# Experts 4 to 7 gated on ScalarE and added by GpSimd, experts 0 to 3 left on VectorE

## The chip, the core and the metric

The kernel runs on one core of a Trainium2 chip. The metric is the device time of one launch in microseconds (us); before the change it was 2887.42 us, the median of three runs (2886.21 to 2891.09). A core has five engines with instruction streams of their own: TensorE multiplies matrices, VectorE and ScalarE work on the 128 partitions of a tile, GpSimd does so more slowly and does not read the accumulation banks here, and SyncE issues the loads and stores. Streams meet in semaphores alone, and each engine takes its instructions strictly in order.

## The reference

Eight images of 128 channels and 48 x 48 positions (2304 tokens) go through one convolutional attention block and one transformer block.

```
x = x + conv_attention(groupnorm(x))        # q, k, v projections, softmax, squeeze-excite
t = tokens(x)
t = t + softmax(LN(t) LN(t)^T) LN(t)        # attention without weights
u = LN(t)
p = softmax(u @ router_w + router_b);  top_p, top_i = top_k(p, 2);  top_p /= sum(top_p)
t = t + sum over the two of top_p * (u @ expert_w[e] + expert_b[e])
```

The kernel computes all 8 experts of each token and weights them with a gate that is zero for the six that were not chosen. A product of two fp32 matrices is three matmuls, of high and low halves (`three`, lines 978 to 980), so nearly every product also costs one ScalarE pass (the high half) and one VectorE pass (the low half).

## The kernel before

The 2304 tokens of an image are 18 tiles of 128; three tiles make a block (384 tokens), so an image has six blocks. One list, `PLAN`, names all steps in order; every engine runs through it and does its own part of each step. So the list sets the order of work on all engines at once.

An image passes two stages. In the first (about 60 to 225 us of the trace for the first image) the scores of the convolutional attention are computed, and no expert step stands in it. In the second (`s1` steps) there are 54 slots. In slot w TensorE does `s1` (six matmuls), then `pv1` of slot w-2 (six matmuls); ScalarE takes the exponential of `s1` (L623) and its high half (L632); VectorE takes the low half (`p1low`, L866, out `pt_lo`). Each slot carries further steps (`beside`): the normalisation and projections of the next image (L530 and L765 for k, L537 and L777 for v), transposes of finished tokens (`o1t`, L873 to L881), and the expert layer of a finished block. For one block that is `uln` (mean and variance, L823 to L830, then a power of -0.5 on GpSimd, L497), one slot later `uapply` (L843, writes `u_tok`), one slot later `ut` (TensorE transposes `u_tok`, L991), one slot later `router`, then six expert steps in six slots, and `yt` (transpose of `acc`, out to memory) three slots after the last of them. The blocks' slots are in `MOE_SLOTS`; `uln` falls in slots 2, 10, 21, 30, 39 and 47, the expert steps in slots 6 to 11, 15 to 20, 26 to 31, 35 to 40, 44 to 49 and 52 to 57. Slots from 54 on are the start of the next image's first stage.

Of the kinds in `SOON` (experts and projections) a step stands ahead of `p1low` in its slot, all other steps behind it.

The six expert steps are two for each tile k: `("expert", b, m, k, 0)` for experts 0 to 3 and `(..., 1)` for experts 4 to 7. Here the first is called half A, the second half B; A stands in a block's first, third and fifth expert slot, B in the second, fourth and sixth. TensorE writes 512 columns (four experts) into one of two accumulation banks that take turns (`ring_bank`); it may write the bank again when the last reader of the step two places earlier on the ring is done (`wait_ring`, `LAST`). VectorE then runs four instructions of 128 columns a half (L951, L954), which alternate between two sums, `acc` and `acc_odd`, and at the end of B adds the two (L962).

## Time and profile before

| | |
|---|---|
| median of three runs | 2887.42 us |
| the profiled execution | 2888.97 us |
| its span in the trace | 2886.8 us |
| granted TensorE clock, mean | 0.98 |
| busy: TensorE, VectorE, ScalarE, GpSimd | 92%, 81%, 65%, 3% |

The profiled execution is 2.2 us longer than its span, and 1.55 us over the median. A busy share is the union of the instructions' spans. Instructions of one engine overlap: a VectorE instruction of 128 columns lasts 340 ns, but the next of a half starts 260 ns after it; matmuls overlap more. In a row of the timeline the first number is the start, the second the length, and a bracket at the end is the idle time of that engine before it and what ended it. Slots are counted here from the `s1` matmuls; rows of single slots are from the second image (b = 1), whose slot 0 begins at 565.8 us.

### The profile page before, as it was taken

How to read it: one execution, taken by the hardware profiler on the slowest of the kernel's cores; microseconds unless marked ns; L12 is line 12 of the kernel's file. 1: busy time of each engine (PE TensorE's matmuls, PEld its weight loads, DVE VectorE, ACT ScalarE, POOL GpSimd, SP SyncE). 2: the span in 40 equal slices, each digit the busy share in tenths (PEclk: the TensorE clock that was granted, in tenths of full speed). 3: DMA queues.
4: the chain of work that ended last, by engine and by line, in shares of the span. 5: the costliest groups of instructions: out<-in, count | busy, mean ns of one | idle time of the engine just before them, and what ended most of it. 6: DMA issues, size and time to landing. Idle time of an engine off the chain costs nothing.

```text
span 2886.8 us, 45014 instructions
## 1 busy us (share of the span) xinstructions
PE 2664.3 (92%) x15334; PEld 2388.0 (83%) x15334; DVE 2324.4 (81%) x6219; ACT 1882.9 (65%) x3729; POOL 90.1 (3%) x120
## 2 busy tenths in 40 slices
PE   5999999999899998999989999999999999899996
PEld 4888978889788897888878798888988889788885
DVE  4886888788887887878878788787888878888777
ACT  2777657666676666767567675676757767577662
POOL 0000000000000000000000000000000000000000
PEclk6999999999999999999999999999999999999998
DMA  1000000000000000000000000000000000000000
GB/s 34 1 1 17 7 6 1 17 7 6 6 1 18 6 6 6 1 18 6 9 4 1 17 7 12 1 1 17 9 9 1 1 20 6 9 1 1 4 9 11
DMA packets 10031, 23.00 MB, mean 8 GB/s; under 512 B 1992, under 2 KB 8528, under 8 KB 8784
## 3 DMA queue, kind: packets, MB, share of 16 engines
q1 hardware_dynamic: 9808, 20.14, 2.0%
q8 instruction: 126, 2.06, 0.3%
q14 instruction: 97, 0.79, 0.1%
HBM read 10.70 MB, written 9.44 MB: 7 GB/s over the span
## 4 chain that ended last, share of the span: by engine, by line
PE 51%; DVE 36%; ACT 6%; issue 6%; SPq 0%; DMA 0%; POOL 0%; ACTq 0%; DVEq 0%; POOLq 0%
PE ps L978 14%; PE ps L980 13%; PE ps L979 13%; PE ps L991 9%; DVE mx L782 6%; DVE pt_lo L866 5%; DVE acc L954 4%; DVE pt_lo L792 3%; DVE acc_odd L954 3%; ACT pt_hi L588 2%; ACT p_rows L576 2%; DVE u_tok L843 1%; DVE acc L962 1%; DVE t_tok L881 1%; ACT pt_hi L632 1%
## 5 line engine op out<-in xcount | busy, mean ns | idle before, releaser
L588 ACT ACTIVATE pt_hi<-ps 128x384 fp32r<-128x384 f32 x864 | 426.0, 493 | 319.7 <-PE ps L991 314.4
L792 DVE TENSOR_TENSOR pt_lo<-ps,pt_hi 128x384 fp32r<-128x384 f32 x864 | 479.2, 556 | 179.6 <-ACT pt_hi L588 171.4
L623 ACT ACTIVATE p_rows<-ps,shift 128x768 f32<-128x768 f32 x432 | 389.2, 901 | 236.7 <-PE ps L980 232.2
L576 ACT ACTIVATE p_rows<-ps,negmax 128x512 f32<-128x512 f32 (+1 forms) x720 | 465.4, 648 | 97.4 <-DVE negmax L786 90.7
L782 DVE TENSOR_REDUCE mx<-ps 128x1 f32<-128x512 f32 (+1 forms) x720 | 441.6, 632 | 70.6 <-PE ps L980 46.5
L991 PE MATMUL ps<-ident,p_rows 128*128 128x128 f32 x2736 | 456.6, 276 | 40.1 <-DVE pt_lo L792 22.9
L866 DVE TENSOR_TENSOR pt_lo<-p_rows,pt_hi 128x768 fp32r<-128x768 f32 x432 | 411.1, 952 | 85.8 <-ACT pt_hi L632 84.0
L991 PEld LDWEIGHTS ps<-ident,p_rows 128*128 128x128 f32 x2736 | 333.9, 141 | 153.1 <-issue 53.0
L632 ACT ACTIVATE pt_hi<-p_rows 128x768 fp32r<-128x768 f32 x432 | 365.5, 846 | 40.4 <-ACT p_rows L623 0.8
L978 PE MATMUL ps<-pt_hi,v_hi 128*128 128x384 f32 x864 | 358.3, 415 | 2.6 <-ACT y_out L597 2.6
L978 PE MATMUL ps<-xt_hi 128*128 128x384 f32 x864 | 306.7, 355 | 0.0
L978 PE MATMUL ps<-k_hi,q_hi 128*128 128x512 f32 (+1 forms) x720 | 277.9, 386 | 29.8 <-ACT p_rows L576 28.5
L978 PE MATMUL ps<-pt_hi,tn_hi 128*128 128x384 f32 x864 | 293.6, 340 | 9.8 <-ACT y_out L597 7.6
L980 PE MATMUL ps<-xt_hi,xt_lo 128*128 128x384 f32 x864 | 292.6, 339 | 0.0
L979 PE MATMUL ps<-xt_lo,xt_hi 128*128 128x384 f32 x864 | 292.4, 338 | 0.0
L980 PE MATMUL ps<-pt_hi,v_lo 128*128 128x384 f32 x864 | 291.5, 337 | 0.0
L980 PE MATMUL ps<-pt_hi,tn_lo 128*128 128x384 f32 x864 | 290.3, 336 | 0.0
L979 PE MATMUL ps<-pt_lo,v_hi 128*128 128x384 f32 x864 | 290.2, 336 | 0.0
L979 PE MATMUL ps<-pt_lo,tn_hi 128*128 128x384 f32 x864 | 290.0, 336 | 0.0
L979 PE MATMUL ps<-k_lo,q_hi 128*128 128x512 f32 (+1 forms) x720 | 273.3, 380 | 0.0
L980 PE MATMUL ps<-k_hi,q_lo 128*128 128x512 f32 (+1 forms) x720 | 272.8, 379 | 0.0
L978 PEld LDWEIGHTS ps<-pt_hi,tn_hi 128*128 128x128 f32 x864 | 163.0, 189 | 20.6 <-issue 13.0
(160 smaller groups left out, 4744.6 us busy)
## 6 DMA issues: line engine op xcount, KB each, us to landing
x_chan<-x SPq DMA_DIRECT2D x8, 1152.0 KB, 5.1
y<-y_out SPq DMA_DIRECT2D x48, 192.0 KB, 1.9
p_rows<-ew SPq DMA_DIRECT2D x1, 512.0 KB
p_rows<-eb SPq DMA_DIRECT2D x1, 512.0 KB
p_rows<-wq SPq DMA_DIRECT2D x1, 64.0 KB
p_rows<-wk SPq DMA_DIRECT2D x1, 64.0 KB
p_rows<-wv SPq DMA_DIRECT2D x1, 64.0 KB
w_sb<-w SPq DMA_DIRECT2D x2, 4.0 KB
```

What stands on the lines that cost most here:

```text
L576: act.activation(p_rows[:, ROW_BUFFER[r, n % 2], a:a + w], ps[:, c, 0:w], ACT.Exp, bias=negmax[:, r % 2:r % 2 + 1], accum_out=dparts[:, n, ...
L588: act.activation(pt_hi[:, slot, :], ring_bank(step)[:, 0:BW], ACT.Copy)\
L623: act.activation(p1_f[:, w % 2, :].rearrange("p (s w) -> p s w", s=2), ps[:, 2 * (w % 2):2 * (w % 2) + 2, 0:BW], ACT.Exp, bias=shift[:, :])\
L632: act.activation(p1_hi[:, w % 3, :], p1_f[:, w % 2, :], ACT.Copy).then_inc(p1_hi_ready, 1)
L782: link(dve.tensor_reduce(mx[:, c:c + 1], ps[:, c, 0:QC[c][1]], AX.X, ALU.max))
L792: dve.tensor_tensor(pt_lo[:, slot, :], ring_bank(step)[:, 0:BW], pt_hi[:, slot, :], ALU.subtract).then_inc(pt_lo_ready, 1)
L866: dve.tensor_tensor(p1_lo[:, w % 3, :], p1_f[:, w % 2, :], p1_hi[:, w % 3, :], ALU.subtract).then_inc(p1_lo_ready, 1)
L954: ins = dve.scalar_tensor_tensor(out=(even, odd)[i % 2], in0=term, scalar=gate, in1=total, op0=ALU.mult, op1=ALU.add)
L978: pe.matmul(out, lhs_hi, rhs_hi, start=start, stop=False)
L979: pe.matmul(out, lhs_hi, rhs_lo, start=False, stop=False)
L980: return pe.matmul(out, lhs_lo, rhs_hi, start=False, stop=stop)
L991: ins = pe.transpose(ring_bank(step)[:, k * 128:(k + 1) * 128], src(k), ident[:, :])
```

## The change

The B half becomes a step of its own kind, `scaled`, in the same slot. TensorE does what it did. VectorE has no part in it: it gates experts 0 to 3 of a tile (half A), two into `acc` and two into a second sum that now lies in `terms`. ScalarE multiplies each of experts 4 to 7 by its gate with one instruction (four of 128 columns) into `terms`, which lies in rows that the first stage uses. GpSimd then adds: term 0 + 1, term 2 + 3, `acc` + the second sum, (0+1) + (2+3), and the total into `acc`. `terms` has two places that tiles take in turns, so VectorE and ScalarE wait for the tile two before (`tile_added`). The bank of a B half is free when ScalarE is done (`terms_ready`), `yt` now waits for `tile_added`, and `scaled` stands in `SOON` as `expert` does.

```diff
-        s.setdefault(slot, []).append(("expert", b, m, i // 2, i % 2))
+        s.setdefault(slot, []).append((("expert", "scaled")[i % 2], b, m, i // 2))
...
+        terms = p_rows[:, 2, 0:2 * 5 * 128].rearrange("p (s a w) -> p s a w", s=2, a=5)
...
+                if kind == "scaled":
+                    m, k = step[2:]
+                    term = [terms[:, (m + k) % 2, i, :] for i in range(5)]
+                    total, paired = acc[:, k, :], at(terms_paired, *step) * 4 - 4
+                    pool.wait_ge(terms_ready, at(terms_ready, *step))
+                    pool.tensor_tensor(term[0], term[0], term[1], ALU.add).then_inc(terms_paired, 1)
+                    pool.tensor_tensor(term[2], term[2], term[3], ALU.add).then_inc(terms_paired, 1)
+                    pool.wait_ge(expert_added, at(expert_added, "expert", b, m, k))
+                    pool.tensor_tensor(total, total, term[4], ALU.add).then_inc(terms_paired, 1)
+                    pool.wait_ge(terms_paired, paired + 2)
+                    pool.tensor_tensor(term[0], term[0], term[2], ALU.add).then_inc(terms_paired, 1)
+                    pool.wait_ge(terms_paired, paired + 4)
+                    pool.tensor_tensor(total, total, term[0], ALU.add).then_inc(tile_added, 1)
...
+                elif kind == "scaled":
+                    m, k = step[2:]
+                    act.wait_ge(ring_full, filled(step))
+                    if k == 0:
+                        act.wait_ge(gates_ready, at(gates_ready, "router", b, m))
+                    earlier = tile_before(b, m, k, 2)
+                    if earlier:
+                        act.wait_ge(tile_added, at(tile_added, "scaled", *earlier))
+                    for e in range(E // 2):
+                        ins = act.activation(terms[:, (m + k) % 2, e, :], ring_bank(step)[:, e * 128:(e + 1) * 128],
+                                             ACT.Identity, scale=gates[:, m % 2, k, E // 2 + e:E // 2 + e + 1])
+                    ins.then_inc(terms_ready, 1)
...
+                    sums = acc[:, k, :], terms[:, (m + k) % 2, 4, :]
                     for e in range(E // 2):
...
-                    if half == 1:
-                        dve.wait_ge(vector_chain, chained(step, links[0]))
-                        dve.tensor_tensor(even, even, odd, ALU.add).then_inc(expert_added, 1)
...
-                    pe.wait_ge(expert_added, at(expert_added, "expert", b, m, TPB - 1, 1))
+                    pe.wait_ge(tile_added, at(tile_added, "scaled", b, m, TPB - 1))
```

VectorE, one image of the second stage, from the last half before `uln` to `uapply` of the same block (slots 39 and 40 of the first image). `u_raw`, `u_mv`, `u_ve` are the variance, `pt_lo` is `p1low`, `u_tok` is what `uapply` writes. Before:

```order
441 L866 TENSOR_TENSOR pt_lo<-p_rows,pt_hi 128x768
442 L823 BN_STATS u_raw<-t_tok 128x6 x3
443 L826 MEMSET wait_carrier 128x1
444 L828 BN_AGGR u_mv<-u_raw 128x2 x3
445 L830 TENSOR_SCALAR u_ve<-u_mv 128x3
446 L954 SCALAR_TENSOR_TENSOR acc<-ps,gates,acc 128x128
447 L954 SCALAR_TENSOR_TENSOR acc_odd<-ps,gates,acc_odd 128x128
448 L954 SCALAR_TENSOR_TENSOR acc<-ps,gates,acc 128x128
449 L954 SCALAR_TENSOR_TENSOR acc_odd<-ps,gates,acc_odd 128x128
450 L962 TENSOR_TENSOR acc<-acc,acc_odd 128x128
451 L866 TENSOR_TENSOR pt_lo<-p_rows,pt_hi 128x768
452 L843 TENSOR_SCALAR u_tok<-t_tok,u_mv,u_rs 128x128 x3
```

and in the changed kernel (L902 is the old L866, L859 to L866 the old L823 to L830, L879 the old L843):

```order
412 L902 TENSOR_TENSOR pt_lo<-p_rows,pt_hi 128x768
413 L859 BN_STATS u_raw<-t_tok 128x6 x3
414 L862 MEMSET wait_carrier 128x1
415 L864 BN_AGGR u_mv<-u_raw 128x2 x3
416 L866 TENSOR_SCALAR u_ve<-u_mv 128x3
417 L902 TENSOR_TENSOR pt_lo<-p_rows,pt_hi 128x768
418 L879 TENSOR_SCALAR u_tok<-t_tok,u_mv,u_rs 128x128 x3
```

The five instructions of half B between `u_ve` and `p1low` are gone. GpSimd, the same image around the power of `uln` in slot 47 (L518, the old L497), where before the powers of an image's blocks followed each other with nothing between:

```order
59 L515 TENSOR_TENSOR acc<-acc,p_rows 128x128
60 L508 TENSOR_TENSOR p_rows<-p_rows 128x128
61 L509 TENSOR_TENSOR p_rows<-p_rows 128x128
62 L511 TENSOR_TENSOR acc<-acc,p_rows 128x128
63 L513 TENSOR_TENSOR p_rows<-p_rows 128x128
64 L515 TENSOR_TENSOR acc<-acc,p_rows 128x128
65 L518 TENSOR_TENSOR u_rs<-u_ve,minus_half 128x3
66 L508 TENSOR_TENSOR p_rows<-p_rows 128x128
```

Rows 60 to 64 are the additions of the tile whose B half stands in slot 47 itself, so here the power is queued right behind them; for the other blocks the tile ahead of the power is of the slot before. ScalarE, slots 40 and 41 (L681 is the new instruction, L647 and L656 the old L623 and L632, L558 the old L537):

```order
326 L647 ACTIVATE p_rows<-ps,shift 128x768
327 L656 ACTIVATE pt_hi<-p_rows 128x768
328 L681 ACTIVATE p_rows<-ps,gates 128x128 x4
329 L647 ACTIVATE p_rows<-ps,shift 128x768
330 L656 ACTIVATE pt_hi<-p_rows 128x768
331 L558 ACTIVATE v_hi<-ps 128x384
```

The four new instructions stand behind the high half of their own slot and ahead of the exponential of the next.

## Rows read from the trace of the kernel before

**Rows 1.** The page: busy time and share of each engine.

```profile
PE 2664.3 (92%) x15334; PEld 2388.0 (83%) x15334; DVE 2324.4 (81%) x6219; ACT 1882.9 (65%) x3729; POOL 90.1 (3%) x120
```

**Rows 2.** Waits of TensorE, whole span: total us, times, longest.

```profile
PE ps L991 <- DVE u_tok L843: 58.0, 48, 4.1
```

**Rows 3.** Waits of TensorE from 589 to 735 us, second image.

```profile
PE ps L991 <- DVE u_tok L843: 4.5, 5, 1.3
PE ps L1008 <- DVE gs L718: 1.1, 1, 1.1
...
PE ps L978 <- DVE acc L962: 0.4, 1, 0.4
...
PE ps L1003 <- DVE gn_mv L710: 0.2, 1, 0.2
```

**Rows 4.** Waits of TensorE from 2708 to 2836 us, last image.

```profile
PE ps L991 <- DVE u_tok L843: 8.8, 5, 2.2
```

**Rows 5.** Timeline of VectorE, 693.5 to 699.3 us, slots 39 to 41.

```profile
695.63 0.17 DVE L830 TENSOR_SCALAR u_ve<-u_mv 128x3 f32<-128x3 f32 x1
695.71 0.35 DVE L954 SCALAR_TENSOR_TENSOR acc<-ps,gates,acc 128x128 f32<-128x128 f32 x1
...
697.08 0.95 DVE L866 TENSOR_TENSOR pt_lo<-p_rows,pt_hi 128x768 fp32r<-128x768 f32 x1
697.95 0.85 DVE L843 TENSOR_SCALAR u_tok<-t_tok,u_mv,u_rs 128x128 f32<-128x128 f32 x3
```

**Rows 6.** Timeline of TensorE, same stretch.

```profile
697.19 0.28 PE L979 MATMUL ps<-w_lo,xg_hi 128*128 128x128 f32 x1
697.30 0.27 PE L980 MATMUL ps<-w_hi,xg_lo 128*128 128x128 f32 x1
698.86 0.55 PE L991 MATMUL ps<-ident,u_tok 128*128 128x128 f32 x3 [1.28 <-DVE u_tok L843]
```

**Rows 7.** Timeline of ScalarE, same stretch.

```profile
692.82 0.91 ACT L623 ACTIVATE p_rows<-ps,shift 128x768 f32<-128x768 f32 x1 [0.96 <-PE ps L980]
693.82 0.85 ACT L632 ACTIVATE pt_hi<-p_rows 128x768 fp32r<-128x768 f32 x1
```

**Rows 8.** Timeline of VectorE and ScalarE, 637 to 641 us, slot 22.

```profile
638.33 0.61 DVE L765 SCALAR_TENSOR_TENSOR k_lo<-ps,biases,k_hi 128x384 fp32r<-128x384 f32 x1
```
```profile
637.51 0.56 ACT L530 ACTIVATE k_hi<-ps,biases 128x384 fp32r<-128x384 f32 x1
```

**Rows 9.** Timeline of VectorE and TensorE, slots 47 to 49.

```profile
721.99 0.34 DVE L954 SCALAR_TENSOR_TENSOR acc<-ps,gates,t_tok 128x128 f32<-128x128 f32 x1
...
723.89 0.85 DVE L843 TENSOR_SCALAR u_tok<-t_tok,u_mv,u_rs 128x128 f32<-128x128 f32 x3
```
```profile
724.80 0.55 PE L991 MATMUL ps<-ident,u_tok 128*128 128x128 f32 x3 [1.20 <-DVE u_tok L843]
```

**Rows 10.** Groups of ScalarE: shapes, count, busy us, mean ns.

```profile
L658 ACT ACTIVATE y_out<-ps,minus_one 128x384 f32<-128x384 f32 x48 | 27.3, 568 | 14.8 <-PE ps L991 14.8
L647 ACT ACTIVATE gexp<-centred 128x24 f32<-128x24 f32 x48 | 10.7, 223 | 91.6 <-DVE centred L900 91.6
```

**Rows 11.** Groups of GpSimd.

```profile
L497 POOL TENSOR_TENSOR u_rs<-u_ve,minus_half 128x3 f32<-128x3 f32 x48 | 41.5, 864 | 1235.6 <-DVE u_ve L830 1235.6
L465 POOL MEMSET ident<- 128x128 f32 x1 | 0.2, 204 | 0.3 <-POOLq L1174 0.3
L477 POOL TENSOR_SCALAR_AFFINE_SELECT group<-group 128x128 f32<-128x128 f32 x1 | 0.5, 523 | 0.0
```

**Rows 12.** Timeline of ScalarE and TensorE at the turn to the third image.

```profile
746.67 0.69 ACT L576 ACTIVATE p_rows<-ps,negmax 128x512 f32<-128x512 f32 x1 [4.13 <-DVE negmax L786]
```
```profile
747.50 0.50 PE L978 MATMUL ps<-k_hi,q_hi 128*128 128x512 f32 x1 [1.39 <-ACT p_rows L576]
```

**Rows 13.** Timeline of GpSimd and VectorE, 244 to 248 us.

```profile
245.15 1.56 POOL L494 TENSOR_TENSOR ln_rs<-ln_ve,minus_half 128x3 f32<-128x3 f32 x1 [23.20 <-DVE ln_ve L830]
```
```profile
245.04 0.96 DVE L866 TENSOR_TENSOR pt_lo<-p_rows,pt_hi 128x768 fp32r<-128x768 f32 x1
```

More of the change, by code:

```diff
@@ L122, in merge @@
         slots.setdefault(slot, []).extend(steps)
-SOON = ("expert", "kproj", "vproj", "qproj")
+SOON = ("expert", "scaled", "kproj", "vproj", "qproj")
 def first_stage(b):
@@ L378, in build @@
         expert_added = signal("expert_added")
+        terms_ready = signal("terms_ready")
+        terms_paired = signal("terms_paired")
+        tile_added = signal("tile_added")
         y_chan_ready = signal("y_chan_ready")
@@ L566, in take @@
                             act.wait_ge(o_added, at(o_added, "ot", b - 1, NB - 1))
+                        if n == 1 and r == 0 and b:
+                            act.wait_ge(tile_added, at(tile_added, "scaled", b - 1, 3, TPB - 1))
                         if n == 1 and r == 1 and b:
@@ L928, in take @@
                 elif kind == "expert":
-                    m, k, half = step[2:]
+                    m, k = step[2:]
                     dve.wait_ge(ring_full, filled(step))
-                    if k == 0 and half == 0:
+                    if k == 0:
                         dve.wait_ge(gates_ready, at(gates_ready, "router", b, m))
@@ L935, in take @@
                             dve.wait_ge(ring_full, filled(("yt", *block_before(b, m))))
-                    if half == 1:
-                        dve.wait_ge(expert_added, at(expert_added, "expert", b, m, k, 0))
-                    even, odd = acc[:, k, :], acc_odd[:, :]
+                    earlier = tile_before(b, m, k, 2)
+                    if earlier:
+                        dve.wait_ge(tile_added, at(tile_added, "scaled", *earlier))
+                    sums = acc[:, k, :], terms[:, (m + k) % 2, 4, :]
@@ L941, in take @@
                     for e in range(E // 2):
-                        i = half * (E // 2) + e
                         term = ring_bank(step)[:, e * 128:(e + 1) * 128]
-                        gate = gates[:, m % 2, k, i:i + 1]
+                        gate = gates[:, m % 2, k, e:e + 1]
                         if e >= 2:
                             dve.wait_ge(vector_chain, chained(step, links[0] - 1))
-                        if i == 1 and k:
-                            dve.wait_ge(expert_added, at(expert_added, "expert", b, m, k - 1, 1))
@@ L950, in take @@
-                        if i == 1:
-                            ins = dve.tensor_scalar(odd, term, gate, None, ALU.mult)
-                        else:
-                            total = residual(m, k) if i == 0 else (even, odd)[i % 2]
-                            ins = dve.scalar_tensor_tensor(out=(even, odd)[i % 2], in0=term, scalar=gate, in1=total,
+                        if e == 1:
+                            ins = dve.tensor_scalar(sums[1], term, gate, None, ALU.mult)
+                        else:
+                            ins = dve.scalar_tensor_tensor(out=sums[e % 2], in0=term, scalar=gate,
+                                                           in1=sums[e % 2] if e else residual(m, k),
@@ L1134, in take @@
                     ins.then_inc(ring_full, 1)
-                elif kind == "expert":
-                    m, k, half = step[2:]
+                elif kind in ("expert", "scaled"):
+                    m, k = step[2:]
+                    half = kind == "scaled"
                     wait_ring(step)
```

23 lines of the change are left out of this document (12 added, 11 removed).

## The prediction, made before the changed kernel was run

> **What bounds the kernel now.** The busy shares come first [rows 1]: TensorE 92%, VectorE 81%, ScalarE 65%, GpSimd 3%. So TensorE sets the time, and VectorE counts only where TensorE stands and waits for it. Next the waits of TensorE over the span [rows 2]: 58.0 us in 48 waits for `u_tok`, one per block. Then the same view cut to slots 9 to 53 of one image [rows 3]: 4.5 us for `u_tok` in five waits, 1.1 and 0.2 for the statistics of the next image (L718, L710), 0.4 for `acc`. The last image, which has no next one beside it, waits 8.8 us in its five [rows 4]. These sums are the ceiling, since the change leaves TensorE's own instructions alone. Last the timeline around one such wait, to see what `u_tok` is late for.
>
> **What is removed.** Of each of 144 tiles VectorE loses five instructions. In the timeline they begin at 695.71 and the next `p1low` at 697.08 [rows 5]: 1.37 us of VectorE a tile, 197 us in all (less than the 1.66 us of their added lengths, because they overlap). That is no gain by itself; the gain is what TensorE no longer waits. A wait that goes gives back a little more than its bracket: matmuls start 0.11 us apart but last 0.28 [rows 6], so I add 0.17 us to each.
>
> Slot 41. `u_ve` starts at 695.63, half B and `p1low` follow, `u_tok` starts at 697.95, and TensorE stands 1.28 us until 698.86 [rows 5, 6]. Without B halves VectorE is also no longer a slot behind: the high half of slot 40 is ready at 693.82 + 0.85 = 694.67 [rows 7], while VectorE takes it at 697.08. Ahead of `u_ve` the half B of slot 38 is gone as well: 695.63 - 1.37 = 694.3 at the earliest, and I allow 0.5 since VectorE now waits for its inputs, 694.8. Then 0.17 for `u_ve`, 0.86 for the power on GpSimd [rows 11] and 0.1 between engines: `u_tok` starts at 696.0 and lasts 0.85; TensorE is free for it from 698.86 - 1.28 = 697.6. The whole wait goes: 1.28.
>
> Slot 49. `u_tok` starts at 723.89, TensorE waits 1.20 us [rows 9]. Here half A of slot 48 stays. It began at 721.99 behind a late VectorE; I move it up by 1.1, to where its bank has just been filled, and `u_tok` with it, to 722.8. 1.0 of 1.20 goes, if the power is done by then.
>
> Slot 23. `k_hi` on ScalarE ends at 637.51 + 0.56 = 638.07 and `k_lo`, ahead of `u_tok` on VectorE, starts at 638.33 [rows 8]. VectorE is already up with ScalarE there, and no B half stands between. Only 0.2 of 0.93 us goes.
>
> Slots 12 and 32 hold the rest of the 4.5 us, 1.1 together; both have a half B in the slot of `uapply`. In slot 32 all goes, in slot 12 half: I take 0.9. The wait of 1.1 and the one of 0.2 for the statistics lie behind the same B halves of slots 9 and 11 and go, and the 0.4 for `acc` (a bank that a B half held) goes since ScalarE frees it.
>
> One full image: 1.28 + 1.0 + 0.2 + 0.9 + 1.1 + 0.2 + 0.4 = 5.1, and 6 waits x 0.17 = 1.0, so 6.1 us. Six images (b = 1 to 6): 36.6. The first image lacks slots 6 to 11 and their waits: 3.9. The last: its 8.8 us fall to a floor of about 1.8 (without projections there is less TensorE work ahead of the transposes, and `u_tok` cannot follow the high half faster), with the overlap 7.7. Sum 48.2 us.
>
> **What is added on ScalarE.** Four instructions of 128 columns from the bank, with the gate as a per-row scale. The trace has none; below stands 223 ns (24 columns, no per-row operand), above 568 ns (384 columns, with one) [rows 10]. On a line between the two 128 columns come to 0.32; I take 0.36, as the per-row operand costs the same at any width, and 1.3 us for four, 187 us in all, bounds 0.9 to 2.3. What hides it: ScalarE idles 0.96 us in a slot of 2.8 us until `s1` is done [rows 7], 1.9 in the two slots of a tile. The exponential of the next slot starts up to 0.4 us late and catches up in the next; `pv1` reads it two slots on. At 2.3 us the cover is gone, and each tile would cost up to 0.4: 58 us. I take 0.
>
> The Trainium skill ("ScalarE: Activation LUTs", What ACT_TABLE_LOAD costs) says 186 ns + 0.833 ns a column, 93 ns more for a per-row operand, and a 93 ns overlap. By its figures, an estimate, an instruction is 386 ns and four are 1.3 us; the sum would not move.
>
> **What is added on GpSimd.** Five additions a tile, 720 in all, of a kind that the trace lacks. Below: 204 ns, a fill of the same shape; above: 864 ns, the power of three columns; between them a select of 128 columns at 523 [rows 11]. I take 0.4, near the middle of fill and select, and with the two waits among them 2.2 us from the terms to `tile_added`. Bounds 1.1 to 4.5. Three places depend on it.
>
> First, a power behind additions in GpSimd's order. In four of the five the tile before is of the slot before and is done 3 us or more before `u_ve`. For slot 47 it is of the same slot: terms at about 719.3, additions until 721.5, power until 722.4, just ahead of the 722.8 above. Past 0.45 us an addition, this wait replaces the one removed.
>
> Second, the turn to the next image. There ScalarE idles 4.13 us for the row maximum (`negmax`), at the end of a run of halves and maxima on VectorE, until 746.67, and TensorE 1.39 us behind ScalarE until 747.50 [rows 12]. Three B halves leave this run; half A of the last tile and the last maxima are then held by TensorE filling their banks, and I put the exponential at 745.4, 1.3 earlier, not 3 x 1.37. But `yt` stands ahead of the second row of scores on TensorE and now needs the last addition: terms at 744.7, plus 2.2, so `yt` at 747.05 and the scores at 747.35. Of 1.3 us gained 0.15 are left, 1 us over seven turns.
>
> Third, the tail: the last tile's additions (2.2) replace a half and a sum on VectorE (1.37), +0.8 for each of two blocks, less some 0.8 for `u_tok` of the last block: +0.8, the turn at the end of the last image +0.4.
>
> **Contention.** In one row the power lasts 1.56 us and not 0.86; it begins 0.11 us after a `p1low`, which reads two operands from on-chip memory, and `u_tok` waits for it [rows 13]. So some pairs keep each other out. `p1low` fills a third of a slot; I charge 2 us for additions or `p1low`s that meet where it matters.
>
> The Trainium skill ("SBUF — State Buffer", Who interferes with whom) says that such a VectorE instruction and a GpSimd instruction that reads this memory exclude each other fully, whichever comes second waiting. The row agrees: 0.96 us of `p1low` ends 0.85 us into the power, and the power is 0.70 longer. By that rule VectorE's 432 `p1low`s could wait up to 0.4 us each; it is the second rival.
>
> The sum: 48.2 + 1.0 - 1.2 - 2.0 = 46 us. Against the profiled execution 2888.97 - 46 = 2843. The runs' median is 1.55 lower, 2841.4; I say 2841.5.
>
> **Rivals.**
>
> 1. The additions are slow, and the change loses. Place: GpSimd, ahead of `yt` and of the power of slot 47. At P us an addition the turn comes at 744.7 + 5P + 0.2; at P = 1.0 it costs 2.9 us in each of seven (20), slot 49 loses its gain and 1.8 more (22), the tail 5: 48 + 1 - 48, no change, 2888. From P = 1.1 on it is slower, at 1.3 by some 25 us, 2912. For it: no row has a GpSimd addition, and its 3-column power takes 0.86. Against: fills and selects of 128 columns take 0.2 to 0.5.
>
> 2. Exclusion costs more than 2 us. If each `p1low` in a slot with additions waits 0.4, VectorE still has room in most slots, but `u_tok` follows `p1low` directly: five blocks x 0.4 x 8 = 16 us, and additions stretched by one `p1low` (0.5 at the turn and in slot 47) 10 more. Gain 20, 2868. For: rows 13. Against: of 48 powers of `uln` the mean is 864 [rows 11], so few met.
>
> 3. More goes than I count: the waits of slots 12 and 23 go whole and the turn keeps 1.3 us (additions near 0.2). 1.1 an image and 8 at the turns: gain 63, 2825. Against: rows 8 show slot 23 bound by ScalarE.
>
> 4. ScalarE becomes late (1.3 was too low, or stretches with projections). The gain shrinks to 25, 2863. For: near slots 15 to 20 it also has the next image's high halves. Against: 65% busy, 71% after.
>
> **Chances.** Forecast (gain 35 to 58) 0.58; rivals 2 and 4 together 0.24; rival 3 0.06; rival 1 0.12, of which a third is no change and two thirds slower. The range 2825 to 2870 leaves out rival 1 and the far side of 3. Within 0.2% (5.8 us, what a measurement of this kernel can tell) 0.04, slower 0.08, faster 0.88.
>
> **What would show it.** After: TensorE's wait for `u_tok` near 58 - 31 = 27 us (4.5 - 3.4 an image; the rest in slot 4 and the tail, which have no B half ahead of them), those for L718 gone; VectorE's busy time down by 200, ScalarE's up by 160 to 190; additions of 0.4 us; a power in slot 47 that starts with the last addition's end; TensorE's wait for `acc` at the turns up to about 2 us each, now ended by GpSimd. The forecast is wrong if `u_tok` is waited for as long as before, or if additions last over 0.8.

## The result, and the profile after

The changed kernel takes 2837.66 us, the median of four runs (2836.02 to 2839.72); the kernel before took 2886.97 on the same chip. The ratio is 0.983, with a 95% interval of 0.9817 to 0.9842: 49 us faster. The forecast was 2841.5 in a range of 2825 to 2870. The profiled execution took 2836.02, its span is 2834.2, the mean granted clock 0.984 (before 0.98).

The busy line of the page answers to [rows 1]:

```profile
PE 2636.5 (93%) x15334; PEld 2381.2 (84%) x15334; DVE 2161.3 (76%) x5499; ACT 2023.1 (71%) x4305; POOL 446.9 (16%) x840
```

VectorE is 163 us less busy, ScalarE 140 more, GpSimd 357 more. The waits of TensorE over the whole span (us in total, times, longest) answer to [rows 2]:

```profile
PE ps L1018 <- DVE u_tok L879: 38.6, 33, 4.0
PE ps L1018 <- POOL acc L515: 24.5, 9, 3.5
PE ps L1005 <- ACT p_rows L600: 20.0, 9, 2.7
PE ps L1035 <- DVE gs L754: 0.6, 1, 0.6
```

The same view of the kernel before, for the three of them that were not shown:

```profile
PE ps L978 <- ACT p_rows L576: 28.5, 16, 2.6
PE ps L991 <- DVE acc L962: 8.9, 9, 1.9
PE ps L1008 <- DVE gs L718: 7.4, 7, 1.1
```

`u_tok` fell from 58.0 to 38.6 (the forecast had 27) and the statistics (`gs`) to almost nothing. `acc` rose from 8.9 to 24.5, and GpSimd now ends it; the nine waits are seven turns and the two output transposes after the last scores.

The groups by shape of what was added (busy us, mean ns, then idle time before it):

```profile
L681 ACT ACTIVATE p_rows<-ps,gates 128x128 f32<-128x128 f32 x576 | 163.0, 366 | 40.2 <-PE ps L1007 36.9 <-DVE gates L961 2.6
L508 POOL TENSOR_TENSOR p_rows<-p_rows 128x128 f32<-128x128 f32 x144 | 85.2, 592 | 767.3 <-ACT p_rows L681 767.3
L513 POOL TENSOR_TENSOR p_rows<-p_rows 128x128 f32<-128x128 f32 x144 | 65.9, 458 | 0.0
L515 POOL TENSOR_TENSOR acc<-acc,p_rows 128x128 f32<-128x128 f32 x144 | 75.2, 522 | 11.3
L518 POOL TENSOR_TENSOR u_rs<-u_ve,minus_half 128x3 f32<-128x3 f32 x48 | 52.2, 1088 | 259.2 <-DVE u_ve L866 259.2
```

ScalarE's instruction takes 366 ns, four take 163.0 / 144 = 1.13 us. A GpSimd addition takes 458 ns undisturbed (L513); the first of a tile (L508) is the one most often disturbed, 40 of its 144 are longer, and its mean is 592. The power of `uln` (L518) took 864 ns before and takes 1088 now: a cost that the change did not bring in by an instruction of its own.

The timeline around slot 12 of the image that begins at 558.3 us (start, length, in brackets the idle time before) shows where it comes from:

```profile
593.14 0.17 DVE L866 TENSOR_SCALAR u_ve<-u_mv 128x3 f32<-128x3 f32 x1
593.21 0.95 DVE L902 TENSOR_TENSOR pt_lo<-p_rows,pt_hi 128x768 fp32r<-128x768 f32 x1
594.91 1.30 DVE L879 TENSOR_SCALAR u_tok<-t_late,u_mv,u_rs 128x128 f32<-128x128 f32 x3 [0.36 <-POOL u_rs L518]
593.38 1.49 POOL L518 TENSOR_TENSOR u_rs<-u_ve,minus_half 128x3 f32<-128x3 f32 x1 [2.72 <-DVE u_ve L866]
596.27 0.55 PE L1018 MATMUL ps<-ident,u_tok 128*128 128x128 f32 x3 [1.07 <-DVE u_tok L879]
```

Half B used to stand between `u_ve` and `p1low` [rows 5]. Now `p1low` is right behind `u_ve` and runs until 594.16, and the power ends 0.71 us after that, 0.63 later than with its usual length. The three instructions of `u_tok` take 1.30 us instead of 0.86, with additions beside them. TensorE still waits 1.07, and 0.63 + 0.44 are all of it. In slot 49 [rows 9] half A stands there, and nothing is in the way:

```profile
709.54 0.86 POOL L518 TENSOR_TENSOR u_rs<-u_ve,minus_half 128x3 f32<-128x3 f32 x1
709.78 0.95 DVE L902 TENSOR_TENSOR pt_lo<-p_rows,pt_hi 128x768 fp32r<-128x768 f32 x1
710.64 0.86 DVE L879 TENSOR_SCALAR u_tok<-t_tok,u_mv,u_rs 128x128 f32<-128x128 f32 x3
711.56 0.55 PE L1018 MATMUL ps<-ident,u_tok 128*128 128x128 f32 x3
```

The turn at the end of the same image answers to [rows 12]:

```profile
731.07 0.45 POOL L508 TENSOR_TENSOR p_rows<-p_rows 128x128 f32<-128x128 f32 x1 [1.56 <-ACT p_rows L681]
732.83 0.45 POOL L515 TENSOR_TENSOR acc<-acc,p_rows 128x128 f32<-128x128 f32 x1
731.78 0.69 ACT L600 ACTIVATE p_rows<-ps,negmax 128x512 f32<-128x512 f32 x1 [0.79 <-DVE negmax L822]
733.34 0.55 PE L1018 MATMUL ps<-ident,acc 128*128 128x128 f32 x3 [2.50 <-POOL acc L515]
```

The exponential is 1.32 us earlier behind the start of slot 53 than before, and the output transpose waits 2.50 us for the fifth addition.

Measured from the start of one slot to the next, in the profiled executions of before and after, images 1 to 6 are 7.2 us shorter on average, from 4.8 to 9.8: slots 49, 41, 32, 19 and 12 give 1.14, 0.95, 0.94, 0.81 and 0.64, slots 9, 11, 17, 23 and 50 together 1.65, slots 13 to 15 together 0.5, the turn with the next first stage 0.65; slot 20 takes 0.34 back. Image 0 gives 4.2, the last image up to its last slot 5.6. The end behind it is 3.5 longer. The first 230 us, in which nothing was changed, are 3.3 shorter: that much is between runs. Sum: 43.0 + 4.2 + 5.6 - 3.5 + 3.3 = 52.6.

Not all of this is a wait that went. In images 1 to 4 the second stage is 5.8 to 6.1 us shorter, in 5 and 6 it is 8.1 and 7.2, and what is more lies in slots 12 to 15. A row of the next view shows a stretch, its length, the busy time of TensorE, its weight load, VectorE, ScalarE and GpSimd, and then the granted TensorE clock. Slots 13 and 14 of image 4 before, of image 5 before, of image 5 after:

```profile
1658.42:1663.88 5.46, 5.46 (x38) 5.18 (x37) 3.27 (x11) 2.96 (x5) 0.56 (x1) 1.00 0.00 0
2011.02:2019.63 8.61, 8.61 (x39) 8.24 (x37) 5.52 (x19) 4.30 (x6) 0.56 (x1) 0.60 0.00 0
1976.64:1982.10 5.46, 5.46 (x38) 5.18 (x37) 3.55 (x11) 2.96 (x5) 1.58 (x2) 1.00 0.00 0
```

From 2012.2 on the granted clock was 0.5 (1.2 of 2.4 GHz) for 6.8 us: the same work took 3.15 us longer, of which slot 15 gave 1.03 back. TensorE had just waited 1.13 us for `gs` and 0.33 for `u_tok` in slot 12. In the trace of before and in that of the load put back (the first experiment) the clock falls so in the second stage of three of eight images each, five of these six times behind the waits of slot 12; in the twelve traces of the other kernels here it does so in none of 96. So it is likely, and not shown, that a part of the gain comes from a clock that no longer falls. At the turns it falls for 0, 3.4 or 6.8 us, which scatters those of the changed kernel by 2.6 us. From slot 53 to the next slot 0, a turn without it takes 182.6 us before (the only one) and 182.3 after (two): 0.3 of the 0.65. Put together, 3.3 us in images 5 and 6, 1.2 in slot 33 of the last image and 2.6 at the turns, some 7 of the 52.6, lie in the clock.

### The profile page after: what moved, and what is told of

The parts are those of the page before. It is cut to its first block, busy times and chain, and to the rows that moved or that the text cites. A ratio compares the mean times of both kernels' runs of the same rounds, so it can differ in the third digit from the quotient of the medians.

```text
span 2834.2 us, 45738 instructions
## 1 busy us (share of the span) xinstructions
PE 2636.5 (93%) x15334; PEld 2381.2 (84%) x15334; DVE 2161.3 (76%) x5499; ACT 2023.1 (71%) x4305; POOL 446.9 (16%) x840
## 4 chain that ended last, share of the span: by engine, by line
PE 61%; DVE 23%; ACT 9%; issue 5%; POOL 2%; SPq 0%; DMA 0%; ACTq 0%; DVEq 0%; POOLq 0%
PE ps L1005 17%; PE ps L1007 17%; PE ps L1006 17%; PE ps L1018 9%; DVE mx L818 6%; DVE pt_lo L828 3%; DVE pt_lo L902 3%; ACT pt_hi L612 2%; ACT p_rows L600 2%; DVE u_tok L879 1%; ACT p_rows L647 1%; POOL u_rs L518 1%; ACT pt_hi L656 1%; ACT p_rows L681 1%; DVE acc L984 1%
## 5 line engine op out<-in xcount | busy, mean ns | idle before, releaser
L902 DVE TENSOR_TENSOR pt_lo<-p_rows,pt_hi 128x768 fp32r<-128x768 f32 x432 | 413.9, 959 | 124.1 <-ACT pt_hi L656 122.4
L647 ACT ACTIVATE p_rows<-ps,shift 128x768 f32<-128x768 f32 x432 | 389.6, 902 | 119.1 <-PE ps L1007 114.0
L656 ACT ACTIVATE pt_hi<-p_rows 128x768 fp32r<-128x768 f32 x432 | 365.6, 846 | 40.1 <-PE ps L1007 0.7
L1005 PE MATMUL ps<-pt_hi,v_hi 128*128 128x384 f32 x864 | 358.6, 415 | 2.5 <-ACT y_out L621 2.5
L1005 PE MATMUL ps<-xt_hi 128*128 128x384 f32 x864 | 305.2, 353 | 0.0
L1005 PE MATMUL ps<-pt_hi,tn_hi 128*128 128x384 f32 x864 | 292.0, 338 | 9.6 <-ACT y_out L621 7.6
L1005 PE MATMUL ps<-k_hi,q_hi 128*128 128x512 f32 (+1 forms) x720 | 275.4, 382 | 21.3 <-ACT p_rows L600 20.0
L502 POOL TENSOR_TENSOR ln_rs<-ln_ve,minus_half 128x3 f32<-128x3 f32 x48 | 41.8, 872 | 1305.1 <-DVE ln_ve L866 1305.1
```

The source lines that it names most:

```text
L502: pool.tensor_tensor(ln_rs[:, :], ln_ve[:, :], minus_half[:, :], ALU.pow).then_inc(ln_rstd_ready, 1)
L647: act.activation(p1_f[:, w % 2, :].rearrange("p (s w) -> p s w", s=2), ps[:, 2 * (w % 2):2 * (w % 2) + 2, 0:BW], ACT.Exp, bias=shift[:, :])\
L656: act.activation(p1_hi[:, w % 3, :], p1_f[:, w % 2, :], ACT.Copy).then_inc(p1_hi_ready, 1)
L902: dve.tensor_tensor(p1_lo[:, w % 3, :], p1_f[:, w % 2, :], p1_hi[:, w % 3, :], ALU.subtract).then_inc(p1_lo_ready, 1)
L1005: pe.matmul(out, lhs_hi, rhs_hi, start=start, stop=False)
```

## The experiments

Theory: the gain is VectorE's time in front of `u_tok`, and what it lost again is the additions' latency at the turns and the end, and GpSimd and VectorE shutting each other out. Rivals: the gain is the earlier release of the result bank; ScalarE's room is what limits it. Each edit is made to the changed kernel, and gains and losses by slots are those of the profiled executions. Times of one call share their runs of the kernel before: 2885.13 us beside the first four, 2882.50 beside the next four, 2885.43 beside the last.

**VectorE's load put back.**

```diff
+                elif kind == "scaled":
+                    for i in range(3):
+                        dve.bn_stats(load_raw[:, i, :], ew_hi[:, 0:384].bitcast(F32))
```

> On top of the change, VectorE reads 384 constant SBUF columns three times in every `scaled` step (bn_stats, about 0.47 us each, 1.4 us a tile), which is as long as the half that the change took from it (1.37 us), in the same place of its order. Nothing reads what it writes. The additions still run on ScalarE and GpSimd. Theory (the gain is VectorE's time ahead of u_tok, k_lo and p1low): nearly all of the 49 us goes, 2878 to 2895 us, with u_tok waits of about 58 us back and the additions' own cost on top. Rival (the gain is ScalarE reading the four results at once and the bank coming free sooner, not VectorE's time): stays within 10 us of 2838. Rival (it is VectorE's accesses to the result bank that went): between the two, near 2860.

2897.81 us, ratio to before 1.0047 (1.0029 to 1.0064): 12.7 us slower than before, 60 slower than the changed kernel. The waits of TensorE over the span:

```profile
PE ps L1025 <- DVE u_tok L881: 62.4, 48, 4.1
PE ps L1025 <- POOL acc L517: 24.5, 9, 3.5
PE ps L1042 <- DVE gs L756: 7.6, 7, 1.2
```

and the group of the load:

```profile
L970 DVE BATCH_NORM_STATS2 load_raw<-ew_hi 128x6 f32<-128x384 f32 x432 | 211.7, 545 | 0.0
```

211.7 / 144 = 1.47 us a tile, 0.1 more than was removed. The load reads constants and waits for no bank, and the banks of the B halves are still freed by ScalarE. The waits that the change was meant to remove are back, 48 for `u_tok` and 7 for `gs`, with `acc` at 24.5 on top. TensorE's waits for a result bank (matmul lines L978 and L1005 of before and after, ended by the gating) went from 8.2 us in 13 to 3.0 in 2 by the change, and are 9.2 in 10 here. So the gain is VectorE's time: nothing of it is left without that. A small part for the earlier release of the bank is not excluded, since the load is 14 us longer in all than what was removed and the additions cost some 16 (next run), where the kernel is 12.7 slower than before.

**One addition instead of five.**

```diff
-                    pool.tensor_tensor(term[0], term[0], term[1], ALU.add).then_inc(terms_paired, 1)
-                    pool.tensor_tensor(term[2], term[2], term[3], ALU.add).then_inc(terms_paired, 1)
...
-                    pool.tensor_tensor(total, total, term[4], ALU.add).then_inc(terms_paired, 1)
-                    pool.tensor_tensor(term[0], term[0], term[2], ALU.add).then_inc(terms_paired, 1)
```

> GpSimd does one addition a tile instead of five (total += first term): experts 1, 3, 5, 6 and 7 of each tile are left out of the sum. VectorE and ScalarE do all that they did. Theory (the additions cost time in two ways: the output transpose waits for the last of them, 24.5 us in the changed kernel, most of it at the turns, and they make VectorE's SBUF work and the power before u_tok longer): 10 to 25 us faster than the changed kernel, 2813 to 2828, the wait of the output transpose on acc under 8 us, VectorE busy some 15 to 30 us less. Rival (the waits on acc only take the place of waits on p_rows or u_tok which come back): within 5 us of 2838.

This kernel leaves experts 1, 3, 5, 6 and 7 out of the sum. 2821.76 us, ratio 0.978 (0.9764 to 0.9796): four additions a tile cost the changed kernel some 16 us. The waits of TensorE over the span:

```profile
PE ps L1012 <- DVE u_tok L873: 31.3, 27, 4.1
PE ps L999 <- ACT p_rows L594: 25.2, 16, 2.6
PE ps L1012 <- POOL acc L509: 8.7, 9, 1.8
```

By slots 6.2 us of it lie behind the start of the last slot, 1.0 at a turn, 0.32 in each of slots 12 and 41 per image. The power's mean is still 1.09 us here, so the additions are not what makes it long. Part of what `acc` gives up (15.8) goes over to `p_rows` (5.2): behind the transpose stood the row maximum.

**ScalarE with twice the instructions.**

```diff
-                    for e in range(E // 2):
+                    for e, c in [(e, c) for e in range(E // 2) for c in (0, 64)]:
...
```

> ScalarE scales each of the four results in two halves of 64 columns: eight instructions a tile instead of four, the same terms. If eight take about 2.0 us where four took 1.13, ScalarE has about 0.9 us more a tile, 126 us in all. Theory (ScalarE has room beside its exp in the slots that count): the terms come 0.9 us later and exp of the next slot up to 0.9 later, which costs at the turns and in few slots: 3 to 15 us slower than the changed kernel, 2841 to 2853, and the waits on p_rows grow from 20 to under 35 us. Rival (the change left ScalarE with no room, the rival on the late ScalarE of the prediction): most of 126 us shows in the slots with tiles, over 25 us slower, 2863 or more.

2866.43 us, ratio 0.9936 (0.9921 to 0.9951), 29 slower than the changed kernel. Here the rival's time came. Slot 49 of a later image:

```profile
1067.15 1.74 ACT L681 ACTIVATE p_rows<-ps,gates 128x64 f32<-128x64 f32 x8
1065.38 1.05 DVE L903 TENSOR_TENSOR pt_lo<-p_rows,pt_hi 128x768 fp32r<-128x768 f32 x1
1065.15 0.47 POOL L515 TENSOR_TENSOR acc<-acc,p_rows 128x128 f32<-128x128 f32 x1
1065.57 1.57 POOL L518 TENSOR_TENSOR u_rs<-u_ve,minus_half 128x3 f32<-128x3 f32 x1
1068.10 0.55 PE L1019 MATMUL ps<-ident,u_tok 128*128 128x128 f32 x3 [1.00 <-DVE u_tok L880]
```

Eight take 1.74 us where four took 1.13. The additions of the tile before end 0.4 us later, the power behind them in GpSimd's order then begins after `p1low` instead of before it, and 0.4 us become 0.9 in this slot (0.94 an image). The rest: slot 20 +0.75, slots 18 and 19 +0.41, slot 38 +0.57, the turn +0.57. In slots 20 and 38 TensorE waits 0.49 us for ScalarE's copy of the sums of finished tokens (L663, ahead of the transposes `o1t`), so there it is ScalarE itself that is late. In all, 88 us more of ScalarE cost 29, though it was idle 29% of the time: my reading of the cover (0.96 us idle in a slot) was right for the slots that I looked at, and too kind as a rule.

**A guard between `u_ve` and `p1low`, long and short.**

```diff
+                    if kind == "uln":
+                        dve.memset(guard[:, :], 0.0)          # long: 128x256
...
+                        for i in range(3):                    # short: 128x3, three times
+                            dve.tensor_scalar(guard[:, i, :], minus_half[:, :], LN_EPS, None, ALU.add)
```

> VectorE sets 128x256 columns of a buffer that nothing reads right behind u_ve, before the next two-operand p1low. Theory (with the half B gone, p1low begins right behind u_ve and before GpSimd's power, which then takes 1.49 instead of 0.86 us since the two shut each other out): the power behind u_ve takes 0.86 us again in slots 12, 23 and 41, u_tok comes up to 0.6 us earlier there, less the guard's own length (some 0.2 to 0.3 us of p1low's); 0 to 8 us faster than the changed kernel, 2830 to 2838. Rival (the power is long for another reason, its operands or the queue on GpSimd): its mean stays 1.09 us and the time is the same or 1 to 4 us longer by the guard.

> Behind u_ve of `uln` VectorE computes three columns three times into a buffer that nothing reads (three instructions like u_ve, about 0.16 us each and some 0.1 apart), so that p1low begins some 0.3 us later and the power has begun. The long guard (256 columns in one instruction) held the power off itself: 1.71 us where it had been 1.49. Theory (the power is slow in slots 12 and 41 because a p1low that began 0.17 us before it keeps it from SBUF, and any long VectorE instruction on SBUF would): with the small guard the power takes 0.86 us there, its mean falls from 1.09 to under 1.0, u_tok comes about 0.4 us earlier in slots 12 and 41, u_tok waits fall from 38.6 to about 34, time 0 to 6 us under the changed kernel's. Rival (the power is long because p1low runs beside it at any time, whoever begins first): mean of the power stays 1.09 or more, time the same or up to 3 us longer.

Long: 2844.70 us, ratio 0.9858 (0.9844 to 0.9873). Short: 2846.83, ratio 0.987 (0.9853 to 0.9888). Both are slower than the changed kernel, and the power's mean rose to 1160 ns in both. Slot 12 with the short guard:

```profile
597.86 0.30 DVE L871 TENSOR_SCALAR guard<-minus_half 128x3 f32<-128x3 f32 x3
598.07 0.95 DVE L906 TENSOR_TENSOR pt_lo<-p_rows,pt_hi 128x768 fp32r<-128x768 f32 x1
598.03 1.70 POOL L519 TENSOR_TENSOR u_rs<-u_ve,minus_half 128x3 f32<-128x3 f32 x1 [2.71 <-DVE u_ve L867]
```

The power now begins first, by 0.04 us here and 0.10 with the long guard, and still takes 1.70: its end is again 0.71 us behind `p1low`'s (599.02). The remedy failed: by slots, 12 and 41 are each 0.2 us longer with either guard, and slot 49 is 0.3 longer with the short one. It is not enough that the power's record begins first. Nor is it the lead that decides. In slot 4 of the same two executions the power began 0.04 to 0.06 us (short guard) and 0.10 us (long) ahead of `p1low` and took 0.85 all 14 times; in slots 12, 23, 32 and 41, with the same leads, it took 1.70 or 1.71 all 34 times. One thing that differs is that GpSimd had been idle for 21 us in slot 4 and for 2.0 to 2.9 us in the others. Whether that is the cause stays open.

**Expert slots moved so that half A covers the power.**

```diff
-MOE_SLOTS = [(2, range(6, 12), 14), (10, range(15, 21), 23),
-             (21, range(26, 32), 34), (30, range(35, 41), 43),
+MOE_SLOTS = [(2, range(7, 13), 14), (10, range(15, 21), 23),
+             (21, range(27, 33), 34), (30, range(36, 42), 43),
```

> Three of the six groups of expert slots go one slot later (7 to 12, 27 to 32, 36 to 41), so that in slots 11, 31 and 40, between u_ve and p1low, VectorE gates experts 0 to 3 (1.03 us, from PSUM) where it had nothing to do. Theory (the slow power comes from the p1low right behind u_ve; and a half of VectorE's gating that stands there covers it): the power takes 0.86 us in those slots and u_tok is then bound by VectorE's own order, about 0.3 us later behind u_ve than now, while TensorE has another 0.7 us of expert matmuls in front of it; waits on u_tok fall by 3 to 8 us, the time by 0 to 8 us. Rival (the tiles' work is merely moved and its new neighbours, among them exp beside ScalarE's four in slots 12, 32 and 41 and the output transpose one slot nearer to the last addition, cost more): 3 to 15 us slower, with new waits on acc.

2848.60 us, ratio 0.9875 (0.9861 to 0.9891): the theory was right on the power, the rival on the time, though no new wait on `acc` came (24.6). Slot 12:

```profile
597.94 0.86 POOL L518 TENSOR_TENSOR u_rs<-u_ve,minus_half 128x3 f32<-128x3 f32 x1
598.35 0.95 DVE L902 TENSOR_TENSOR pt_lo<-p_rows,pt_hi 128x768 fp32r<-128x768 f32 x1
599.59 0.85 ACT L656 ACTIVATE pt_hi<-p_rows 128x768 fp32r<-128x768 f32 x1
600.35 1.14 ACT L681 ACTIVATE p_rows<-ps,gates 128x128 f32<-128x128 f32 x4
601.63 0.52 PE L1018 MATMUL ps<-ident,u_tok 128*128 128x128 f32 x3 [1.21 <-ACT p_rows L681]
```

With half A between `u_ve` and `p1low`, the power begins 0.41 us ahead of `p1low` and takes 0.86; its mean over the kernel fell from 1088 to 875, the waits for `u_tok` from 38.6 to 26.1. So it is shown that the power is long when `p1low` stands right behind `u_ve`. But in slot 12 the transposes now wait 1.21 us for ScalarE, whose four terms hold the bank of the ring that they need and stand behind an exponential and a high half. There a half on ScalarE in the slot of `uapply` takes the place of the wait that it removes. This is not what makes the kernel slower: by slots the first group even gains 0.4 us an image. The other two lose 1.4 and 0.4, and TensorE's new waits there are 0.65 us for `p1low` in slot 27 and 0.52 for `v_lo` in each of slots 32 and 41.

**The output transpose one slot later at the turn.**

```diff
-             ... (47, [52, 53, 54, 55, 56, 57], 60)]
+             ... (47, [52, 53, 54, 55, 56, 57], 61)]
```

> The output transpose of the block that ends at the turn goes one slot later in the order (61 instead of 60), behind one more group of scores. In the changed kernel it waits for the last addition there, 2.5 to 3.5 us of TensorE each, 24.5 us in nine waits. Theory (that wait is the price of the additions' latency at the turn and can be covered by the scores behind it): the waits on acc fall from 24.5 to under 12 us, about 1 to 2 us at each of seven turns, 5 to 13 us under the changed kernel. Rival (behind the transpose stands a wait for exp that ends no earlier, so the wait only moves: p_rows grows by what acc loses): within 3 us of 2838.

2833.20 us, ratio 0.9826 (0.9808 to 0.9844), where the changed kernel beside its own runs of before has 0.9836 (last table): not told apart by time alone. Its waits over the span:

```profile
PE ps L1005 <- ACT p_rows L600: 34.0, 16, 2.7
PE ps L1018 <- POOL acc L515: 7.1, 2, 3.5
```

and the scores of the turn in the timeline:

```profile
733.26 0.50 PE L1005 MATMUL ps<-k_hi,q_hi 128*128 128x512 f32 x1 [1.77 <-ACT p_rows L600]
```

Of 17.4 us that `acc` gives up 14.0 appear as waits for the row maximum's exponential. A turn in which the granted clock does not fall takes 181.6 us (two of them), where the changed kernel has 182.3: 0.7 us a turn.

**Two additions in one instruction of 256 columns.**

```diff
-                    pool.tensor_tensor(term[0], term[0], term[1], ALU.add).then_inc(terms_paired, 1)
-                    pool.tensor_tensor(term[2], term[2], term[3], ALU.add).then_inc(terms_paired, 1)
+                    pair = [terms[:, (m + k) % 2, i:i + 2, :] for i in (0, 2)]
+                    pool.tensor_tensor(pair[0], pair[0], pair[1], ALU.add).then_inc(terms_paired, 1)
```

> GpSimd adds terms 0 and 1 to terms 2 and 3 in one instruction of 256 columns and then the two sums: four instructions a tile instead of five (same result to rounding). If an instruction of 256 columns takes about 0.46 us plus what 128 more columns cost (0.2 to 0.4), the chain of a tile ends 0.1 to 0.4 us earlier. Theory (GpSimd's time is per instruction for a part, and the tile's latency counts only at the turns and the end): 1 to 4 us under the changed kernel, waits on acc down by 1 to 3 us. Rival (GpSimd's time goes by columns alone, 0.42 a 128, so nothing is saved and the first addition starts no earlier): within 1 us of the changed kernel.

2843.25 us, ratio 0.9858 (0.9841 to 0.9875): no gain, rather a loss of about 6 (every run is slower than every run of the changed kernel). The group of the new instruction, and its shortest, median and longest in ns:

```profile
L509 POOL TENSOR_TENSOR p_rows<-p_rows 128x256 f32<-128x256 f32 x144 | 124.8, 866 | 785.4 <-ACT p_rows L681 785.4
L509 POOL TENSOR_TENSOR p_rows<-p_rows x144: 722/737/1955, 303.2 to 2838.1; 128x256 f32<-128x256 f32 x144
```

The wait of TensorE for `u_tok` over the span became

```profile
PE ps L1018 <- DVE u_tok L879: 44.3, 41, 4.1
```

The mean of 866 ns contains the disturbed ones; undisturbed it is 737 ns for 256 columns against 458 for 128, so a part of the time is per instruction, as the theory had it. From the first addition's start to the last one's end a tile takes 2.12 us in the median and not 2.26, and the waits on `acc` fell from 24.5 to 23.4. The gain is lost elsewhere: slots 12 and 41 are each 0.27 us longer, where additions meet `u_tok` (waits 44.3 against 38.6).

**The last blocks on VectorE, alone, with the later transpose, and with the first group of slots moved.** The control is the changed kernel itself.

```diff
+def late(step):
+    return step[0] == "scaled" and step[1] == B - 1 and step[2] >= 4
...
+                elif late(step):                              # VectorE
...
+                    for e in range(E // 2):
...
+                        ins = dve.scalar_tensor_tensor(out=sums[e % 2], in0=ring_bank(step)[:, e * 128:(e + 1) * 128],
+                                                       scalar=gates[:, m % 2, k, E // 2 + e:E // 2 + e + 1],
+                                                       in1=sums[e % 2], op0=ALU.mult, op1=ALU.add)
...
+                    dve.tensor_tensor(sums[0], sums[0], sums[1], ALU.add).then_inc(tile_added, 1)
```

> The changed kernel itself, unchanged, beside the three that follow, so that effects of a few us are read against it on the same chip. Both theories: 2832 to 2842 us.

> Only the last image's blocks 4 and 5 (six tiles, after the last scores) are gated by VectorE alone, with two running sums as in the kernel before; all other tiles as in the changed kernel. Theory (past the last scores VectorE has room and the chain ScalarE's four terms, then five additions of 0.46 us, is longer than VectorE's half: the end of the kernel lost 3.5 us by the change): 3 to 6 us faster than the changed kernel, all of it behind the last s1, with the two waits on acc there (7 us) falling to under 3. Rival (at the end the chain through u_tok and the router sets the time, whoever gates): within 1.5 us.

> The late output transpose at the turn (61 instead of 60) and the last blocks on VectorE, together. Theory (two losses at different places, both from the additions' latency): their gains add, 6 to 12 us under the changed kernel, near 2828, waits on acc under 3 us in all. Rival (either gain is noise between chips): within 3 us of the changed kernel.

> As the one before, and the expert slots of the first of the six groups go one slot later (7 to 12), the only one of the three shifted groups whose slots came out shorter when all three were shifted (slots 6, 8 and 12 together 0.4 us an image, against +1.4 and +0.4 in the other two). Theory (the power in slot 12 is covered by VectorE's half from PSUM, at no new wait): another 2 to 4 us, power mean 1.02 instead of 1.09 us. Rival (what moved is only counted elsewhere): 0 to 3 us slower than the one before.

| kernel | median us | ratio to before (95%) |
|---|---|---|
| changed kernel again | 2837.25 | 0.9836 (0.9823 to 0.9850) |
| last blocks on VectorE | 2836.02 | 0.9830 (0.9817 to 0.9844) |
| and the transpose at 61 | 2832.00 | 0.9811 (0.9798 to 0.9825) |
| and slots 7 to 12 | 2829.33 | 0.9805 (0.9791 to 0.9819) |

Three small steps in the expected direction, none of which stands clear of the next by its interval; only the last kernel is clear of the control, by 8 us. It beats both kernels of this case. By the medians the first step gives 1.2 us, which is what its rival said, and the first two together 5.3, between theory and rival. In the profiled executions the end behind the start of the last slot is 2.2 us shorter than the control's with VectorE alone in the last blocks, and 1.5 and 1.9 shorter in the next two kernels. The waits on `acc` there fell from 7 to 5.6, not under 3: 3.5 us of it belong to the block before, which GpSimd still adds. The waits of the last kernel:

```profile
PE ps L1029 <- ACT p_rows L605: 32.3, 16, 2.7
PE ps L1042 <- DVE u_tok L884: 29.4, 26, 3.8
PE ps L1042 <- ACT p_rows L686: 7.2, 6, 1.2
```

The last step moved a wait rather than removed it: the kernel one line above waits 36.7 us for `u_tok`; here 29.4 are left and 7.2 for ScalarE's terms came in. By the slots it gains 0.4 us an image.

## Why the forecast held, step by step

- **VectorE is what counts.** Right, and shown by the load put back: the time, 48 waits for `u_tok` and 7 for `gs` return. Its busy time fell by 163 us and not by 197. The lengths of its instructions sum to 221 us less, where the removed ones made 240: 19 us are other instructions that last longer now, half of it `u_tok` (65 of its 144 take 0.47 to 0.50 us instead of 0.34, beside an addition). The other 15 us are overlap: neighbours that followed each other directly covered 307 us of one another before, 249 now.
- **Slot 41** was to give 1.28 + 0.17 and gave 0.95. The step that failed is "0.86 for the power": in image 1 `p1low` began with it at 683.68 and it took 1.68; `u_tok` started at 685.40. I had moved the half away and not asked what would then be next behind `u_ve`.
- **Slot 49**: forecast 1.17, measured 1.14. The power was behind the additions in GpSimd's order, as said, and just in time.
- **Slot 23**: forecast 0.37, measured 0.21. **Slot 32** gave 0.94 for a wait of 0.74.
- **Slot 12** is a wait handed on. TensorE waited 1.13 for `gs` there and then 0.33 for `u_tok`. I counted the 1.13 as gained in full and half of the 0.33 too. `gs` went, TensorE came to `u_tok` that much earlier and now waits 1.07 for it: the slot gave 0.64. All of the 1.07 is contention (the power 0.63, `u_tok` 0.44 longer).
- **Statistics and `acc`, elsewhere**: slot 11 gave 0.40 for the bracket of 0.17, slot 19 gave 0.81 for the 0.4 of `acc`. The 0.17 added to each wait was too little there. Slots 9, 17 and 50 gave 1.04 that I had not priced, since no bracket stood there: in slot 9 TensorE was idle for 0.13 us, too little for the list of waits, and the next matmuls started 0.41 later than without it. Slot 20 took 0.34.
- **Per image**, 6.1 was forecast without the turn. Images 1 to 4, with the clock up, gave 6.0, by misses in both directions. **The last image** was to give 7.7 and gave 5.6, of which 1.2 is clock. I had put its floor at 1.8 us of waits; 4.8 are left, 1.10 to 1.24 in each of slots 12, 23, 32 and 41. With the moved slots the long power is gone there, and slots 12, 32 and 41 of the last image are 0.49 shorter each, though 0.7 us of expert matmuls moved into each of them: a part of that floor is contention.
- **Contention** was charged with 2 us, the term most out of size. Of the waits left, 1.07 in slot 12 and 0.3 to 0.5 in slot 41 are contention, some 8 us over six images. By the groups' means the additions lost 33 us over 0.46 each and the power 48 x 0.224 = 11, most of it off the path. Rival 2 (each `p1low` 0.4 later) had the wrong victim: `p1low` took 0.959 in the mean, only 12 of 432 more than 1.0 (up to 1.23), and it was GpSimd and `u_tok` that became longer.
- **ScalarE's instruction**: 0.36 forecast, 0.366 measured; four in 1.13, not 1.3. Busy time up by 140, where 160 to 190 was forecast, as instructions overlap their neighbours. "I take 0" for its effect held, but not as safely as I wrote: 0.61 us more a tile already cost 29 us. By the figures of the Trainium skill ("ScalarE: Activation LUTs", What ACT_TABLE_LOAD costs) an instruction is 386 ns, an estimate; the trace has 366.
- **GpSimd's addition**: 0.40 forecast, 0.458 measured, starts 0.42 apart. From the terms to `tile_added` 2.2 was forecast; from 731.07 to 733.28 are 2.21.
- **The turn**: the exponential 1.3 earlier was forecast; from slot 53 it starts 1.32 earlier (13.21 us before, 11.89 after), and the scores behind `yt` 0.29 where I had 0.15. The whole turn gave 0.3 where the clock did not fall.
- **The tail**: 1.2 forecast, 3.5 in this pair of executions and 2.6 in the control's; the granted clock was 0.5 there for 24.7 us before, for 33.1 and 29.5 in these two. With the last blocks back on VectorE 0.4 of the 2.6 is left (1.1 and 0.6 in the two kernels built on it), and with one addition a tile the tail is 2.7 shorter than before. So the additions' chain is the cause and was mis-sized.

The profiled pair differs by 53 us where the sum said 46. Without the untouched first 230 us (3.3) and the clock (some 7) it is 42.4: the last image gave 3.3 less, the tail cost 2.3 more, images 1 to 6 gave 0.6 and image 0 0.5 less, the turns 1.1 more, and the 2.0 charged for contention are already in the slots. So the medians, 3.8 us from the forecast, look better than the steps are: misses of both signs, and a clock that the forecast had no term for. How much of the medians' 49 us is clock no trace shows, as only one execution of each kernel was traced. Rivals 1 and 3 did not happen; rival 2 did so in part, with another victim; the run with eight ScalarE instructions shows rival 4 a short way off.

The Trainium skill ("SBUF — State Buffer", Who interferes with whom) says that a VectorE instruction with two SBUF inputs contends with a GpSimd one that reads SBUF, and that single-input ones do so only in the modes that use both port pairs, which `tensor_scalar` can enter. The traces agree on who meets whom: `p1low` (two inputs) and `u_tok` (`tensor_scalar`) meet GpSimd, the halves that read the result banks do not (342 ns beside an addition and without). The prediction took from it that whichever comes second waits. For the power the traces have that in one order only. When `p1low` began 0.17 us ahead, the power ended 0.71 us behind it. When the power began 0.24 us ahead, as in slot 49 above, the two ran side by side for 0.62 us and took 0.86 and 0.95, their usual lengths.

## What to carry to other kernels

When an instruction goes, look up what then stands directly behind its neighbour: here a two-input VectorE pass moved up against a GpSimd step on the critical chain, and kept 0.3 to 0.5 of 1.3 us of wait in one slot; in another a wait of 1.07 stands where 1.13 for something else had gone. Work handed to idle engines is paid in latency where someone waits for its last piece, so hand over the tiles in the middle and keep the ones at a turn or at the end. A wait of the bound engine that is cut often hands its time to the one behind it: read what released the next instruction before counting the whole bracket. Before a difference between two traces is put down to the change slot by slot, lay the granted clock beside it.

## What was not expected of the hardware

- GpSimd's fp32 addition takes 458 ns for 128 columns and 737 for 256, undisturbed. The power of three columns takes 0.85 to 0.86 us.
- In slots 12 and 41 the power ended 0.71 or 0.72 us after `p1low` whether it had begun 0.17 us after it (1.49), together with it (1.68), or 0.04 or 0.10 before it (1.70, 1.71). In slot 4, with 0.03 us of lead, it took 0.85, and `p1low` 0.98:

```profile
568.64 0.85 POOL L518 TENSOR_TENSOR u_rs<-u_ve,minus_half 128x3 f32<-128x3 f32 x1 [21.00 <-DVE u_ve L866]
568.67 0.98 DVE L902 TENSOR_TENSOR pt_lo<-p_rows,pt_hi 128x768 fp32r<-128x768 f32 x1
```

- Halving ScalarE's instructions from 128 to 64 columns takes the mean from 366 to 328 ns; eight in a row take 1.74 us, four of double width 1.13.
- At a granted clock of 0.5 the work of slots 13 and 14 took 3.15 us longer, and in five of six cases in a second stage the clock fell behind waits of 1.5 to 2.1 us in one slot.
